# Causal attention in a decoder kernel: the row maximum from half the products, two heads side by side in the array

## The chip, the cores and the metric

One Trainium2 chip, one core. The metric is the device time of one execution in microseconds (us); smaller is better. The kernel is a whole decoder pass of six layers; the change touches one of them, the causal self-attention.

## The reference, cut to what matters

```python
B, S, D, H, DH = 2, 1024, 256, 16, 16
q, k, v = (xn @ Wqkv + bqkv) split by head          # xn: layer norm of x
score = einsum('bhqd,bhkd->bhqk', q, k) * DH ** -0.5
score = where(causal, score, -inf)                  # tril
p = softmax(score)                                  # float32
x = x + (p @ v) @ Wout + bout
```

A softmax row may be shifted by any number near its maximum without changing what it gives, apart from rounding; the kernel uses that below.

## The kernel before

Products in float32 accuracy are made from bf16 parts. Each of q and k is split into three bf16 parts that add up to the float32 value (high, middle, low), and six of the nine part products are kept. `Q_PART` and `K_PART` list them, and the parts of one head are stacked under each other in 6 x 16 = 96 partitions, so that one bf16 matmul with 96 rows sums all six.

The work goes in 8 steps: a step is one batch and a quad of 4 heads. A step does three things.

1. Pieces (`piece`, L1422, with the causal mask added on the diagonal block by a 128-column matmul of `ident16` and `future`, L1425). They are the scores with queries on the partitions, made only for the row maximum. For query tile qi (128 queries) and each half of up to 512 keys there is a matmul for each head; a piece fills one PSUM bank of 512 columns, with as many heads in it as fit (4 heads at 128 keys, 2 at 256, 1 at 384 or 512). VectorE takes the maximum (`reduce`, L1583).
2. The shift. VectorE negates the maxima and splits them into two bf16 parts (`split_shift`, L1594 to L1599), TensorE turns them (`turn_shift`, L1432), VectorE copies them to `stage` (L1606), and two DMAs put them into rows 96 and 97 of the q stack (`keep_shift` on SP, L1332), where k has ones.
3. Scores with keys on the partitions (`scores`, L1444, mask L1447), 98 rows, so that the shift is already subtracted; ScalarE's exp (L1543); and the product with v (`values`, L1459: float32, 128 rows by 32 columns, 4 heads side by side in the array). Then `turn_out` (L1468) and `norm` (L1611, L1613). At the end of a batch come `turn_batch` (L1476), `add_bias` (L1619), `project` (L1484) and `finish` (L1625).

The order is written out by hand and is the same on every engine. The unit is one head with 512 columns: a step has 4 x 9 = 36 units of pieces and as many of scores. `count_pieces` sets `upto`: after each score slot the pieces are issued that bring their sum to `done + 36` units, so that the maxima run one whole step ahead of the scores; at the very start it is `11 + 3.5 * done` for the first 10 units, to catch up. Each engine runs its own list in order: TensorE that waits for one thing holds back all that follows.

PSUM has 8 banks: 3 for scores, one for the output of `values`, and a ring of 4 single banks for everything else (pieces, shifts, turned outputs, projections). A tile of the ring is written when the one 4 earlier has been read (`tile`).

The stacks come from DRAM. `loads(n)` on SP issues 12 DMAs of 128 KB for step n, into one of three buffers; the third (`qs[2]`, `ks[2]`) lies in spent weights and needs the projections of the second batch to be done, and a memset of its ones by GpSimd (L1372), which TensorE waits for before the first piece (`k_ones`(2)). The order on SP is: stores of the parts of batch 0; loads(0), loads(1), keep_shift(0), loads(2); then keep_shift(hs) for each half step, and loads(n+2) after the second half of step n. Before the loads of step 3 stand 6 stores of 512 KB, the parts of batch 1.

```python
aim = 11 + 3.5 * done if done < 10 else done + 36
upto.append(max(upto[-1], sum(a <= aim for a in sums)))
```

```python
score = lambda slot: c.bank(slot % SCORES)
out_tile = c.bank(SCORES)
ring_bank = lambda what: c.bank(SCORES + 1 + nth[what] % TILES)
```

Of the kernel before, what the change touches and what calls it, by code (L numbers as in the profile page):

```python
# [1181 lines left out]

def score_pieces():

    out = []
    for qi in range(TT):
        for half, first in enumerate(range(0, (qi + 1) * P, CH)):
            n = min(CH, (qi + 1) * P - first)
            per = min(QUAD, CH // n)
            out += [(qi, first, n, list(range(h, h + per)), half) for h in range(0, QUAD, per)]  # L1190
    return out


def causal_attention_layer(nc, c):
# [10 lines left out]
    SCORES, TILES = 3, 4  # L1205
# [3 lines left out]
    LATER = 6  # L1209
# [21 lines left out]
    def count_pieces():  # L1231

        size = [len(heads) * n / CH for _, _, n, heads, _ in pieces] * STEPS
# [26 lines left out]
    with ExitStack() as ctx:  # L1260
# [3 lines left out]
                                       loaded0=0, loaded1=0, loaded2=0, shifted0=0, shifted1=0, made=0, read=0,  # L1264
                                       max_step=0, parts=0, scored=0, expd=0, av=0, out_copied=0, inv=0))
        set_round(0, s)
        loaded = [s["loaded0"], s["loaded1"], s["loaded2"]]
# [20 lines left out]
        spare = c.weights[:, 0:first].bitcast(BF16).rearrange("p (a h n) -> p a h n", a=2, h=QUAD)  # L1288
        qs = [q_stack[:, 0], q_stack[:, 1], spare[:, 0]]
        ks = [k_stack[:, 0], k_stack[:, 1], spare[:, 1]]  # L1290
# [11 lines left out]
        ring_bank = lambda what: c.bank(SCORES + 1 + nth[what] % TILES)  # L1302

        with nc.Block() as block:

            @block.sync
            def _(sync):
                def loads(n):
                    b, quad = divmod(n, QUADS)
                    a = n % 3  # L1310
                    if n == 2:
                        pr["v_proj"].round = 1
                        sync.wait_ge(*pr["v_proj"](4))
                    if n >= 3:
                        sync.wait_ge(*s["scored"](QUAD * first_group(2 * (n - 2))))
                    by_head = lambda ap: ap.rearrange("(h d) n -> d h n", d=DH)
                    rows = slice(quad * QUAD * DH, (quad + 1) * QUAD * DH)
                    for r in range(len(Q_PART)):
                        sync.dma_start(qs[a][r * DH:(r + 1) * DH], by_head(q_dram[b, Q_PART[r], rows, :]))\
                            .then_inc(loaded[a].sem, 16)  # L1320
                        sync.dma_start(ks[a][r * DH:(r + 1) * DH], by_head(k_dram[b, K_PART[r], rows, :]))\
                            .then_inc(loaded[a].sem, 16)

# [4 lines left out]
                def keep_shift(hs):  # L1328
                    _, _, half = part_of(hs)
                    sync.wait_ge(*s["read"](nth["shift", hs] + 1))  # L1330
                    for i in range(SHIFT):
                        sync.dma_start(qs[hs // 2 % 3][ROWS + i:ROWS + i + 1, :, half * CH:(half + 1) * CH],  # L1332
# [7 lines left out]
                loads(0)  # L1340
                loads(1)
                keep_shift(0)
                loads(2)
                for hs in range(1, HALVES):
                    keep_shift(hs)
                    if hs == 3:
                        for n in range(2):
                            sync.wait_ge(*s["later_part"](4 * (n + 1)))
                            for i in range(3):
                                store(1, n, i, s["later_stored"])  # L1350
                    if hs % 2 == 1 and 3 <= hs // 2 + 2 < STEPS:
                        if hs // 2 + 2 == QUADS:
                            sync.wait_ge(*s["later_stored"](6 * 16))
                        loads(hs // 2 + 2)

            @block.gpsimd
            def _(pool):
# [11 lines left out]
                pr["v_proj"].round = pr["q_raw"].round = pr["k_raw"].round = 1  # L1369
# [3 lines left out]
                pool.wait_ge(*s["stored"](6 * 16))  # L1373
                pool.wait_ge(*s["k_ones"](2))
# [11 lines left out]
            def _(pe):  # L1386
# [21 lines left out]
                def tile(what):  # L1408
# [3 lines left out]
                    return ring_bank(what)  # L1412

                def piece(p):
                    n, i = divmod(p, NPC)
                    qi, first, keys, heads, _ = pieces[i]
                    if i == 0:
                        pe.wait_ge(*loaded[n % 3](LOADS * (n // 3 + 1)))
                    bank = tile(("piece", p))
                    diagonal = first + keys == (qi + 1) * P  # L1420
                    for x, h in enumerate(heads):
                        mm = pe.matmul(bank[:, x * keys:(x + 1) * keys], qs[n % 3][0:ROWS, h, qi * P:(qi + 1) * P],  # L1422
                                       ks[n % 3][0:ROWS, h, first:first + keys], start=True, stop=not diagonal)
                        if diagonal:
                            mm = pe.matmul(bank[:, (x + 1) * keys - P:(x + 1) * keys], ident16[:], future[:], start=False, stop=True)  # L1425
                    mm.then_inc(s["made"].sem)

                def turn_shift(hs):
                    rows = tile(("shift", hs))[0:SHIFT * QUAD, :].bitcast(BF16)
# [5 lines left out]
                def scores(slot):  # L1435
                    (hs, ki), h = groups[slot // QUAD], slot % QUAD
                    a, half = hs // 2 % 3, hs % 2
                    if ki == 0 and h == 0:
                        pe.wait_ge(*shifted[hs % 2](SHIFT * 16 * (hs // 2 + 1)))
# [24 lines left out]
                def turn_out(hs):  # L1464
                    bank = tile(("out", hs))
# [5 lines left out]
                def turn_batch(b, x):  # L1471
                    m, half = divmod(x, 2)
                    bank = tile(("turn", b, x))
# [5 lines left out]
                def project(b, x):  # L1479
                    m, j = divmod(x, NCH)  # L1480
                    bank = tile(("project", b, x))
# [12 lines left out]
                pe.wait_ge(*s["k_ones"](2))  # L1494
# [64 lines left out]
            def _(dve):  # L1559
# [20 lines left out]
                def reduce(p):  # L1580
                    qi, _, keys, heads, part = pieces[p % NPC]
                    nh = len(heads)
                    dve.tensor_reduce(mx[:, part, qi, heads[0]:heads[0] + nh],  # L1583
                                      tile(("piece", p))[:, 0:nh * keys].rearrange("p (h n) -> p h n", n=keys), AX, ALU.max)\
                       .then_inc(s["read"].sem)
# [66 lines left out]
        clear_signals(nc, norm_s, pr, s)  # L1652

# [778 lines left out]
```

## Time and profile before

| | |
|---|---|
| time, median of 3 runs | 1981.68 us (1981.13 to 1981.76) |
| the profiled execution: time / span | 1980.98 us / 1979.3 us |
| TensorE (PE) busy | 1722.5 us, 87% of the span |
| VectorE (DVE) busy | 901.5 us, 46% |
| ScalarE (ACT) busy | 628.3 us, 32% |
| pieces, L1422 and L1425 | first at 978.96 us, last at 1232.9 us |
| end of the causal layer's last score | 1262 us |

The times of the trace are from the start of the span. Busy shares over the whole span say little here, since the change touches about 285 us of 1979; the rows below are cut to that stretch. A matmul's duration in the trace includes its way through the array, so matmuls overlap in the list: what one costs in a dense stream is the distance from its start to the start of the next. "128*32" after a matmul is its number of rows and columns in the array, "x4" the number of records; a float32 matmul has two records.

### The profile page before, as it was taken

The numbers are of one execution on the slowest core, as the hardware profiler recorded it, in microseconds if no ns is written. First come the engines' busy times: TensorE is split into PE (matmuls) and PEld (weight loads), VectorE is DVE, ScalarE is ACT, GpSimd is POOL, SyncE is SP. The second block draws the span as 40 slices with busy tenths as digits, with TensorE's granted clock in tenths as the row PEclk, the third lists the DMA queues.
The fourth block names the chain that finished last, engine by engine and source line by source line (L and its number), as shares of the span: only waits on it lengthen the run. The fifth ranks groups of instructions, "written<-read, shape, count | busy, mean of one in ns | idle before, by whom it ended". The sixth has DMA issues, their size and how long they took to land. (4 is left out here: it accounts for less than half of the span.)

```text
span 1979.3 us, 20127 instructions
## 1 busy us (share of the span) xinstructions
PE 1722.5 (87%) x7698; PEld 961.8 (49%) x7698; DVE 901.5 (46%) x1458; ACT 628.3 (32%) x1024; POOL 63.6 (3%) x73
## 2 busy tenths in 40 slices
PE   5797795989999977887799999778866999999998
PEld 3444442443222213333445544335643788888886
DVE  3404404664443323122488777154636636354552
ACT  2312312522222223113247656432323322121220
POOL 0000000000000000003220000000002000000000
PEclk8898897989999998998989999989968999999999
DMA  4001000000000000000626240000021022222201
GB/s 171 0 0 58 0 0 3 0 1 0 1 1 1 0 0 0 0 0 0 128 33 129 34 56 11 4 0 1 0 86 57 1 86 85 86 86 86 85 29 43
DMA packets 27693, 67.48 MB, mean 34 GB/s; under 512 B 3096, under 2 KB 14424, under 8 KB 25176
## 3 DMA queue, kind: packets, MB, share of 16 engines
q1 hardware_dynamic: 27608, 66.33, 12.4%
q8 instruction: 55, 0.90, 0.2%
q14 instruction: 30, 0.25, 0.0%
HBM read 57.80 MB, written 8.39 MB: 33 GB/s over the span
## 5 line engine op out<-in xcount | busy, mean ns | idle before, releaser
L1543 ACT ACTIVATE arena<-psum 128x512 f32<-128x512 f32 (+3 forms) x384 | 164.3, 499 | 123.7 <-PE psum L1447 91.6
L1583 DVE TENSOR_REDUCE b_mx<-psum 128x1 f32<-128x512 f32 (+3 forms) x304 | 181.4, 653 | 45.1 <-PE psum L1425 34.4
L2077 PE MATMUL psum<-m_wo,m_hidden 128*128 128x256 f32 (+1 forms) x704 | 153.4, 379 | 1.0 <-DVE arena L2280 1.0
L2175 ACT ACTIVATE m_gelu<-psum 128x512 f32<-128x512 f32 (+1 forms) x88 | 52.5, 597 | 305.2 <-PE psum L2063 305.2
L2077 PEld LDWEIGHTS psum<-m_wo,m_hidden 128*128 128x128 f32 (+1 forms) x704 | 133.7, 190 | 19.3 <-issue 1.2
L2063 PE MATMUL psum<-m_x_high,m_w_high 128*128 128x512 f32 (+1 forms) x352 | 140.0, 398 | 2.9 <-issue 2.9
L2063 PE MATMUL psum<-m_x_rest,m_w_high 128*128 128x512 f32 (+1 forms) x352 | 138.9, 395 | 0.0
L2063 PE MATMUL psum<-m_x_high,m_w_rest 128*128 128x512 f32 (+1 forms) x352 | 138.5, 393 | 0.0
L874 ACT ACTIVATE x_probs<-psum 128x1024 f32<-128x1024 f32 x64 | 65.5, 1023 | 219.2 <-PE psum L730 219.2
L950 DVE TENSOR_REDUCE x_mx<-psum 128x2 f32<-128x1024 f32 x64 | 77.4, 1223 | 116.6 <-PE psum L704 115.9
L2299 DVE TENSOR_TENSOR m_hidden<-m_gelu,psum 128x512 f32<-128x512 f32 (+1 forms) x88 | 60.5, 687 | 139.5 <-PE psum L2063 139.5
L1444 PE MATMUL psum<-b_q_stack,b_k_stack 98*128 98x512 bf16 (+3 forms) x288 | 91.5, 334 | 7.4 <-DMA b_q_stack<-b_stage 3.0
L1422 PE MATMUL psum<-b_k_stack,b_q_stack 96*128 96x512 bf16 (+3 forms) x288 | 90.3, 345 | 6.1 <-POOL weights_sb L1372 3.7
L743 PE MATMUL psum<-x_probs,arena 128*64 128x512 f32 x256 | 69.1, 617 | 9.8 <-ACT x_out L884 9.8
L2063 PEld LDWEIGHTS psum<-m_x_high,m_w_high 128*128 128x128 f32 (+1 forms) x352 | 65.1, 185 | 19.9 <-issue 3.7
L730 PE MATMUL psum<-arena 64*128 64x512 f32 x256 | 73.2, 649 | 0.0
L2063 PEld LDWEIGHTS psum<-m_x_high,m_w_rest 128*128 128x128 f32 (+1 forms) x352 | 65.1, 185 | 16.4
L2063 PEld LDWEIGHTS psum<-m_x_rest,m_w_high 128*128 128x128 f32 (+1 forms) x352 | 65.1, 185 | 16.2
L1459 PE MATMUL psum<-arena,weights_sb 128*32 128x512 f32 (+3 forms) x768 | 71.7, 492 | 0.0
L414 PE MATMUL psum<-arena,weights_sb 128*128 128x512 f32 x128 | 58.6, 621 | 14.2 <-DVE arena L201 14.2
L704 PE MATMUL psum<-arena 64*128 64x512 f32 x256 | 68.1, 623 | 2.9 <-DVE x_mx L950 1.9
L1109 PE MATMUL psum<-weights_sb 128*128 x96 | 48.9, 635 | 18.0 <-PEq L1087 12.2
(375 smaller groups left out, 2678.9 us busy)
## 6 DMA issues: line engine op xcount, KB each, us to landing
m_w<-w SPq DMA_DIRECT2D x16, 1368.0 KB, 9.1
m_wo<-wo SPq DMA_DIRECT2D x8, 1280.0 KB
weights_sb<-weights SPq DMA_DIRECT2D x2, 2820.0 KB, 9.1
b_q_stack<-b_q_dram SPq DMA_DIRECT2D x36, 128.0 KB, 7.0
b_k_stack<-b_k_dram SPq DMA_DIRECT2D x36, 128.0 KB, 7.5
weights_sb<-weights SPq DMA_DIRECT2D x1, 3328.0 KB, 13.1
b_q_dram<-b_q_parts SPq DMA_DIRECT2D x6, 512.0 KB, 3.3
b_k_dram<-b_k_parts SPq DMA_DIRECT2D x6, 512.0 KB, 4.4
```

The costliest lines, as they stand in the source:

```text
L704: mm = pe.matmul(to[:, h * CH:(h + 1) * CH], qt[b][rows, m, q0:q0 + P], kt_[b][rows, m, first:first + CH], start=True, stop=True)
L730: mm = pe.matmul(to[0:keys, h, :], k, qt[b][rows, m, half * CH:(half + 1) * CH], start=False, stop=True)
L743: mm = pe.matmul(out_tile[h * DH:(h + 1) * DH, :], v, probs[slot % RING][0:keys, h, :], start=(kt == 0), stop=(kt == TT))
L874: ins = act.activation(probs[slot % RING][:], two_heads(units), ACT.Exp, scale=SCALE)
L950: dve.tensor_reduce(mx[:, n % 2, i // 2, i % 2, :], two_heads(tile(("piece", n, i))), AX, ALU.max).then_inc(s["read"].sem)
L1422: mm = pe.matmul(bank[:, x * keys:(x + 1) * keys], qs[n % 3][0:ROWS, h, qi * P:(qi + 1) * P], ks[n % 3][0:ROWS, h, first:first + keys], st ...
L1444: mm = pe.matmul(score(slot)[:, 0:n], ks[a][0:ROWS + SHIFT, h, ki * P:(ki + 1) * P], qs[a][0:ROWS + SHIFT, h, q0:q0 + n], start=True, stop ...
L1459: mm = pe.matmul(out_tile[h * PAD:(h + 1) * PAD, CH - n:CH], v_aug[:, b * TT + ki, quad * QUAD + h, :], probs[(QUAD * (2 * pair + i) + h) ...
L1543: act.activation(probs[slot % RING][:, 0:n], score(slot)[:, 0:n], ACT.Exp, scale=SCALE).then_inc(s["expd"].sem)
L1583: dve.tensor_reduce(mx[:, part, qi, heads[0]:heads[0] + nh], tile(("piece", p))[:, 0:nh * keys].rearrange("p (h n) -> p h n", n=keys), AX, ...
L2063: mm = pe.matmul(c.bank(base + n % 2)[0:H_N(h), :], of[:, k, at], x_of[:, k, :], start=(k == 0 and of is w_high[w] and x_of is x_high), st ...
L2077: mm = pe.matmul(bank[:, q * D:(q + 1) * D], hidden[0:H_N(h), h, (2 * i + q) * P:(2 * i + q + 1) * P], wo[0:H_N(h), h, :], start=(h == 0), ...
```

## The change

- For the pieces only three of the six part products are kept (high x high, high x middle, middle x high): 3 x 16 = 48 rows. Scores keep all six.
- Two heads of a pair are computed side by side: one from partitions 0 to 47, one from partitions 64 to 111, each as a matmul of 48 rows, into two different banks. A piece is now a tile of two banks with one pair of heads (2 x 512 or 2 x 384 columns) or two pairs (at 256 or 128 keys). There are 20 pieces in a step in place of 38. The mask on the diagonal is added as before, by one full matmul for each head.
- The ring has 2 tiles of two banks in place of 4 of one bank; shifts, turned outputs and projections take such a tile too and use one bank of it.
- The maximum is taken from both banks by one instruction (up to 128 x 1024).
- The 48-row stacks are loaded on their own (`firsts(n)`: 12 DMAs of 64 KB), with two buffers in spent weights and in `c.ln`. The 96-row stacks now have two buffers (`stacks(n)`: 12 DMAs of 128 KB); GpSimd's memset of the third is gone. The order on SP: firsts(0), stacks(0), keep_shift(0), stacks(1), firsts(1), then after the second half of step n: stacks(n+1), firsts(n+2). Step 3's stores stay where they were.
- `LATER`, the number of pieces between the last piece of a half step and its `turn_shift`, is 3 in place of 6.

```diff
-Q_PART = (0, 0, 0, 1, 1, 2)
-K_PART = (0, 1, 2, 0, 1, 0)
+Q_PART = (0, 0, 1, 0, 1, 2)
+K_PART = (0, 1, 0, 2, 1, 0)
+FIRST = 3
...
-            per = min(QUAD, CH // n)
-            out += [(qi, first, n, list(range(h, h + per)), half) for h in range(0, QUAD, per)]
+            out += [(qi, first, n, pairs, half) for pairs in (((0,), (1,)) if 2 * n > CH else ((0, 1),))]
...
-    SCORES, TILES = 3, 4
+    SCORES, TILES = 3, 2
+    SIDE = P // 2
...
-    LATER = 6
+    LATER = 3
...
-        size = [len(heads) * n / CH for _, _, n, heads, _ in pieces] * STEPS
+        size = [2 * len(pairs) * n / CH for _, _, n, pairs, _ in pieces] * STEPS
...
-        ring_bank = lambda what: c.bank(SCORES + 1 + nth[what] % TILES)
+        ring_tile = lambda what: c.psum[2 + nth[what] % TILES]
+        ring_bank = lambda what: ring_tile(what)[:, 0:CH]
...
+                def firsts(n):
...
+                    if n == 1:
+                        pr["v_proj"].round = 1
+                        sync.wait_ge(*pr["v_proj"](4))
+                    if n >= 2:
+                        sync.wait_ge(*s["made"](nth["piece", NPC * (n - 1) - 1] + 1))
...
+                    for r in range(FIRST):
+                        for y in range(2):
+                            to = slice(y * SIDE + r * DH, y * SIDE + (r + 1) * DH)
+                            sync.dma_start(q_first[a][to], by_side(q_dram[b, Q_PART[r], rows, :])[y]).then_inc(loaded_first[a].sem, 16)
+                            sync.dma_start(k_first[a][to], by_side(k_dram[b, K_PART[r], rows, :])[y]).then_inc(loaded_first[a].sem, 16)
...
-                loads(0)
-                loads(1)
+                firsts(0)
+                stacks(0)
                 keep_shift(0)
-                loads(2)
+                stacks(1)
+                firsts(1)
...
-                pool.wait_ge(*pr["v_proj"](4))
-                pool.wait_ge(*s["k_ones"](1))
-                pool.memset(ks[2][ROWS:ROWS + SHIFT], 1.0).then_inc(s["k_ones"].sem)
...
-                    for x, h in enumerate(heads):
-                        mm = pe.matmul(bank[:, x * keys:(x + 1) * keys], qs[n % 3][0:ROWS, h, qi * P:(qi + 1) * P],
-                                       ks[n % 3][0:ROWS, h, first:first + keys], start=True, stop=not diagonal)
+                    for x, pair in enumerate(pairs):
+                        for y in range(2):
+                            rows = slice(y * SIDE, y * SIDE + FIRST * DH)
+                            mm = pe.matmul(to[:, y * CH + x * keys:y * CH + (x + 1) * keys], q_first[a][rows, pair, qi * P:(qi + 1) * P],
+                                           k_first[a][rows, pair, first:first + keys], start=True, stop=not diagonal)
                         if diagonal:
-                            mm = pe.matmul(bank[:, (x + 1) * keys - P:(x + 1) * keys], ident16[:], future[:], start=False, stop=True)
+                            for y in range(2):
+                                last = y * CH + (x + 1) * keys
+                                mm = pe.matmul(to[:, last - P:last], ident16[:], future[:], start=False, stop=True)
...
+                    of = ring_tile(("piece", p))[:].rearrange("p (y n) -> p y n", y=2)
...
+                    dve.tensor_reduce(to, of, AX, ALU.max).then_inc(s["read"].sem)
```

## Rows read from the trace of the kernel before

The stretches below give, after their length, the busy us of PE, PE's weight loads, DVE, ACT and GpSimd (with instructions), then the granted clock of PE (1.00 is 2.4 GHz), the DMA share and GB/s.

**Rows 1.** Busy time by engine over one whole step of scores.

```profile
1068.39:1099.84 31.45, 31.14 (x277) 15.74 (x273) 25.17 (x49) 21.15 (x50) 0.00 (x0) 1.00 0.42 52
```

**Rows 2.** Groups by line over three such steps, 1036.95 to 1131.28 us.

```profile
L1422 PE MATMUL psum<-b_k_stack,b_q_stack 96*128 96x512 bf16 (+3 forms) x96 | 29.1, 327 | 0.0
...
L1425 PE MATMUL psum<-b_future,b_ident 128*128 128x128 bf16 x96 | 18.6, 220 | 0.0
...
L1422 PE MATMUL psum<-weights_sb 96*128 96x512 bf16 (+3 forms) x48 | 14.5, 326 | 0.0
```

**Rows 3.** PE in order of time inside a step: start, duration, instruction.

```profile
1103.16 0.22 PE L1425 MATMUL psum<-b_future,b_ident 128*128 128x128 bf16 x1
1103.31 0.39 PE L1432 MATMUL psum<-b_ident,b_shift 128*8 128x128 bf16 x4
1103.63 0.34 PE L1444 MATMUL psum<-b_q_stack,b_k_stack 98*128 98x384 bf16 x1
1103.80 0.22 PE L1447 MATMUL psum<-b_past,b_ident 128*128 128x128 bf16 x1
1103.86 0.33 PE L1422 MATMUL psum<-b_k_stack,b_q_stack 96*128 96x384 bf16 x1
...
1110.36 0.38 PE L1422 MATMUL psum<-b_k_stack,b_q_stack 96*128 96x512 bf16 x1
...
1111.24 0.38 PE L1422 MATMUL psum<-b_k_stack,b_q_stack 96*128 96x512 bf16 x1
```

**Rows 4.** PE in order of time in the cross-attention layer, which has matmuls in row halves.

```profile
521.53 0.39 PE L725 MATMUL psum<-x_shift_t,x_ones 2*128 2x512 bf16 x2
521.85 0.70 PE L730 MATMUL psum<-arena 64*128 64x512 f32 x2
...
522.39 0.60 PE L730 MATMUL psum<-arena 64*128 64x512 f32 x2
522.82 0.60 PE L704 MATMUL psum<-arena 64*128 64x512 f32 x2
...
523.25 0.59 PE L704 MATMUL psum<-arena 64*128 64x512 f32 x2
523.77 0.65 PE L743 MATMUL psum<-x_probs,arena 128*64 128x512 f32 x2
```

**Rows 5.** DVE's maxima: over two banks (cross attention) and over one.

```profile
L950 DVE TENSOR_REDUCE x_mx<-psum 128x2 f32<-128x1024 f32 x64 | 77.4, 1223 | 116.6 <-PE psum L704 115.9
...
L1583 DVE TENSOR_REDUCE b_mx<-psum 128x1 f32<-128x512 f32 x72 | 46.1, 680 | 10.5 <-PE psum L1425 7.6 <-PE psum L1422 2.9
```

**Rows 6.** The start of the layer's pieces, GpSimd and DVE in order of time.

```profile
975.33 0.69 DVE L1573 COPY weights_sb<-psum 128x512 f32<-128x512 f32 x1 [1.03 <-PE psum L1404]
975.35 3.51 POOL L1372 MEMSET weights_sb<- 2x4096 bf16 x1 [35.66 <-PE psum L1404]
...
979.62 6.14 DVE L1583 TENSOR_REDUCE b_mx<-psum 128x4 f32<-128x512 f32 x11 [3.60 <-PE psum L1425]
...
994.40 13.31 DVE L1583 TENSOR_REDUCE b_mx<-psum 128x4 f32<-128x512 f32 x23 [0.35 <-PE psum L1425]
...
1008.26 1.28 DVE L1583 TENSOR_REDUCE b_mx<-psum 128x4 f32<-128x512 f32 x2
```

**Rows 7.** SP's queue at the start: first load, first shift.

```profile
954.99 0.33 SPq L1319 DMA_DIRECT2D b_q_stack<-b_q_dram  x1
...
988.41 1.42 SPq L1332 DMA_DIRECT2D b_q_stack<-b_stage  x2
```

**Rows 8.** The stretch in which loads(2) moves, columns as in Rows 1.

```profile
989.87:1003.30 13.43, 11.48 (x54) 5.28 (x55) 10.79 (x19) 3.86 (x7) 13.10 (x5) 0.73 0.97 118
```

**Rows 9.** The stretch in which loads(3) moves, columns as in Rows 1.

```profile
1050.00:1062.70 12.70, 12.70 (x101) 6.15 (x103) 11.76 (x23) 9.85 (x21) 0.00 (x0) 1.00 1.05 176
```

**Rows 10.** PE's waits for DVE at turn_shift, 1040 to 1170 us (total, times, longest).

```profile
PEld psum L1432 <- DVE b_mx L1583: 2.6, 8, 0.5
```

**Rows 11.** DVE in the layer's tail.

```profile
1267.62 2.73 DVE L1619 TENSOR_SCALAR arena<-psum,vectors_sb 128x512 f32<-128x512 f32 x4 [0.81 <-PE psum L1476]
```

More of the change, by code:

```diff
@@ L1339, in _ @@
                 sync.wait_ge(*s["stored"](6 * 16))
-                loads(0)
-                loads(1)
+                firsts(0)
+                stacks(0)
                 keep_shift(0)
-                loads(2)
+                stacks(1)
+                firsts(1)
                 for hs in range(1, HALVES):
                     keep_shift(hs)
+                    n = hs // 2
                     if hs == 3:
[L1347 to L1352, printed above, removed]
+                        for i in range(2):
+                            sync.wait_ge(*s["later_part"](4 * (i + 1)))
+                            for part in range(3):
+                                store(1, i, part, s["later_stored"])
+                    if hs % 2 == 1:
+                        if 2 <= n + 1 < STEPS:
+                            stacks(n + 1)
+                        if n + 2 == QUADS:
                             sync.wait_ge(*s["later_stored"](6 * 16))
-                        loads(hs // 2 + 2)
+                        if n + 2 < STEPS:
+                            firsts(n + 2)
             @block.gpsimd
@@ L1464, in turn_out @@
                 def turn_out(hs):
-                    bank = tile(("out", hs))
+                    bank = tile(("out", hs))[:, 0:CH]
                     pe.wait_ge(*s["out_copied"](hs + 1))
@@ L1472, in turn_batch @@
                     m, half = divmod(x, 2)
-                    bank = tile(("turn", b, x))
+                    bank = tile(("turn", b, x))[:, 0:CH]
                     pe.wait_ge(*s["read"](nth["out", 2 * QUADS * (b + 1) - 1] + 1))
@@ L1480, in project @@
                     m, j = divmod(x, NCH)
-                    bank = tile(("project", b, x))
+                    bank = tile(("project", b, x))[:, 0:CH]
                     pe.wait_ge(*s["read"](nth["turn", b, 3] + 1))
@@ L1580, in reduce @@
                 def reduce(p):
[L1581 to L1585, printed above, removed]
+                    qi, _, keys, pairs, part = pieces[p % NPC]
+                    dve.wait_ge(*s["made"](nth["piece", p] + 1))
+                    of = ring_tile(("piece", p))[:].rearrange("p (y n) -> p y n", y=2)
+                    if len(pairs) == 1:
+                        of, to = of[:, :, 0:keys], mx[:, part, qi, 2 * pairs[0]:2 * pairs[0] + 2]
+                    else:
+                        of = of[:, :, 0:2 * keys].rearrange("p y (x n) -> p y x n", x=2)
+                        to = mx[:, part, qi, :].rearrange("p (x y) -> p y x", y=2)
+                    dve.tensor_reduce(to, of, AX, ALU.max).then_inc(s["read"].sem)
                 def split_shift(hs):
```

52 lines of the change are left out of this document (29 added, 23 removed).

## The prediction

> **What bounds the layer now.** I read the busy time of one whole step first, cut out from one first score to the next. A step takes 31.45 us; PE is busy 31.14 of it, DVE 25.17, ACT 21.15 [rows 1]. So PE sets the pace, with hardly a gap, and its clock is full; what DVE or ACT saves is worth nothing here until DVE needs over 31 us. Then I read the groups of three such steps: the pieces are 144 matmuls (96 and 48), 48 in a step, and 96 masks, 32 in a step [rows 2]. By the code these 48 carry 36 units of 512 columns.
>
> What PE's instructions cost is their distance in order of time, and not their duration. Four 512-column matmuls start within 1111.24 - 1110.36 = 0.88 us, 0.22 us each; a 128-column one passes in 0.06 us (1103.80 to 1103.86) [rows 3]. A step's pieces are thus 36 x 0.22 = 7.9 us plus 32 x 0.06 = 1.9 us of masks.
>
> **What the change takes away on PE.** A head has 48 rows, and two heads run side by side. Cross attention shows such a pair: the two halves (records x2) of a 512-column bf16 matmul are followed after 0.32 us, and 0.10 of that is another matter, below, so both pass in the 0.22 us of one [rows 4]. 36 units become 18: -3.95 us per step. Masks are full matmuls still, one for each head: no change.
>
> **What it adds on PE: a change of shape in the array.** Wherever the array goes from one division to another, an extra shows:
> - Full to narrow columns, bf16 on both sides: mask to turn_shift 0.15 us (1103.16 to 1103.31) against 0.06: +0.09. Back: 0.32 us for four transposes of 0.056 to 0.06: +0.09 [rows 3].
> - Row halves, float32: L730 to L704, halves on both sides, 0.43 us; L704 to L743, from row halves to full rows, 0.52 us: +0.09. From the 2-row bf16 pair to 64-row pairs 0.32 against 0.22: +0.10 [rows 4].
>
> No row shows a bf16 step from 128 rows to 48 or back. Its bounds are 0 and 0.10; every change of shape in the rows, four kinds of them, costs 0.09 to 0.10, so I take 0.095, and 0.19 to 0.20 for going in and out. How often? In a step there are 8 diagonal and 4 other key spans, two pairs of heads in each: 24 pairs. The masks (full) follow each diagonal pair, also between the two pairs of a four-head piece, and by the written order a score or a mask stands between any two pieces. So 24 entries and 24 exits: 24 x 0.19 to 0.20 = +4.6 to +4.8 us. Net +0.6 to +0.9 us per step; I take +0.75. The point from which it turns is 3.95 / 24 = 0.165 us for in and out together. It is the narrow pairs that lose: a 128-column pair saves 0.06 us and pays 0.19; even a 512-column pair gains only 0.03.
>
> The Trainium skill (TensorEngine Tiling (Array Packing), "Key Properties") says that a change of tiling mode, and not just of tile, drains TensorE. By that rule the charge falls on all 48 changes, as in the sum; by its table "Theoretical Speedup" (up to 2 times for a contraction of at most 64) alone the pieces would gain 3.95 us per step with nothing to pay, the first rival. Rows 4 agree with both, the pair in the time of one and the 0.09 at the border.
>
> It counts where PE sets the pace: the pieces of steps 2 to 7 and some 0.7 of step 1's, 6.7 steps: 6.7 x 0.75 = +5.0 us.
>
> **The ring of two.** DVE's reading of two banks is 1.22 us against 0.68 for one [rows 5]. By durations a step's maxima cost now 30 x 0.68 and 8 (at 384 columns) x some 0.55, 24.8 us, and afterwards 14 of 1024 columns, 4 of 768 and 2 of 512: 14 x 1.22 + 4 x 0.95 + 2 x 0.68 = 22.3 (0.95 and 0.55 lie on the line through the two rows). So DVE's 25.2 us [rows 1] become some 22.7: further from the bound, and worth nothing by itself. But the ring is two deep, and turn_shift must have the tile two back. In the half with full spans the order is: 512-wide pair, score, four-head piece at 128 keys, turn_shift. From the end of the wide pair PE gets there after 0.22 + (0.38 changes + 4 x 0.06 masks + 2 x 0.06) = 0.96 us; DVE needs the matmul's way through the array (0.22 - 0.06 = 0.16 us [rows 3]) and 1.22, 1.4 in all: PE waits about 0.4 to 0.5 us, and by the same count in the other half, where it now waits 2.6 / 8 = 0.3 us each time [rows 10]. So +0.2 each, +0.4 per step; bounds are 0 (ACT lags behind in that half, and what PE loses to DVE it would lose to ACT anyway) and 1.2 (DVE late by one more tile). LATER at 3 two-unit pieces is the same lead as before. I take +0.3: 6.7 x 0.3 = +2.0 us.
>
> The tail and the end of batch 0 use the ring for 4 turns and 4 projections each. There four evictions run back to back in 2.73 us, 0.68 each [rows 11]. With two tiles each turn waits for the read two back, while DVE is at the next: nothing lost if PE fills a tile within 0.68 us, 0.2 if it needs its four transposes and the way through on top. Over 16 of them that is 0 to 3 us; I take +1.0.
>
> **The start.** PE's first piece waits for GpSimd's memset, until 975.35 + 3.51 = 978.86 us [rows 6]. The memset is gone; what is left is DVE's last copy of the projection, 975.33 + 0.69 = 976.02 [rows 6]: -2.8 us. firsts(0), 0.79 MB, starts at 954.99 [rows 7] and at the 118 GB/s of loads(2) [rows 8] is there by 962; stacks(0), 1.57 MB more, by 976, before the first score: both hidden by the projections.
>
> That lead is lost again at the first piece of step 1. DVE sets the pace here: 11, 1, 3 and 23 maxima, the last ending at 994.40 + 13.31 = 1007.71, and step 1 begins at 1008.26 [rows 6], from loads(1), which had come long before. After the change that data is firsts(1), which SP issues behind keep_shift(0) and stacks(1). The first shift goes out at 988.41 [rows 7], afterwards some 2.6 earlier, 985.8; the issue of the stacks from 987.3. loads(2) moved 1.57 MB in 13.4 us [rows 8]; 2.36 MB take 20.1: landed at 1007.4. DVE would want the pieces 2.8 and some 0.4 for fewer maxima before 1007.71, at 1004.5. So PE stands still in front of them for 3 to 4 us, the scores behind it too, and DVE's first maximum of step 1 is at about 1008.3, where it is now. I take +0.3 for what is over (a bound of -2.8 if the two loads overlap better than that, of +3 if the standstill brings the clock down, as the 0.73 of rows 8 shows that this stretch can).
>
> **Later loads.** In a plain step SP issues 24 DMAs in place of 12, 20 us of data, and the next shift's two DMAs queue behind them; from keep_shift of the second half (some 6 units into the next step's pieces) to the next step's scores there are 30 of 36 units, 26 us, so they fit. Only once do the 6 stores come first: loads(3) moves until 1062.70 [rows 9], and in its place stacks(2) and firsts(3) will, the second after the first. 0.79 MB more take 6.7 us: 1069.4, and keep_shift(4) behind it, wanted where the stretch of rows 1 begins, at 1068.39, plus the delay so far. +0.6 us; bounds 0 and 3.
>
> **Sum.** 5.0 + 2.0 + 1.0 + 0.3 + 0.6 = +8.9 us: 1980.98 becomes 1989.9 for the profiled execution, whose span is 1979.3; the median of the runs is 0.7 higher, so 1990.5. Layers after the causal one are only moved.
>
> **Rivals.**
> - Faster, "the change of shape is cheap for bf16 rows": the side-by-side pair keeps its 3.95 us and in and out cost less than 0.165. For it: no row has just this change. Against: four kinds of change all cost the same. If in and out cost 0.10 together: 24 x 0.10 = 2.4, net -1.55 per step, -10.4, and with the other +3.9 the median is 1981.7 - 6.5 = 1975; at nothing the step would be 27.5 us, which DVE's 22.7 allows: 1981.7 - 26.5 + 3.9 = 1959. Chance 0.10.
> - No difference (1977.7 to 1985.6; 0.2%, 4 us, is about what a measurement of this kernel can tell from no change): the changes of shape fall into PE's waits for ACT, which already make some of the step, the ring waits too, and the start keeps part of its 2.8. Step net +0.2 and +1 elsewhere: 1984. Chance 0.15.
> - Slower by more, "the ring is the new bound": each shift waits 0.6 us more, and double pieces hold back scores so that ACT then lacks work: +1.5 a step in place of 0.3, +8: 1998.5. For it: DVE is at 80% in a step [rows 1], and a tile's read holds PE up nearly twice as long [rows 5]. Against: it has slack on average, and the lead of PE in units is the same. Chance 0.20.
> - Forecast: 0.55, own range 1986 to 1995.
>
> Slower 0.75, same 0.15, faster 0.10. The range leaves out most of the faster case and the end of the ring case: 1981 to 2001.
>
> **What the profile afterwards should show.** The pieces' matmuls x384 as 48*128, in pairs that start together; 0.31 us from a 512-wide pair to the next full matmul, 0.15 from a mask to the next pair. Maxima x160 with a mean near 1.1 us. A step of 32.2 to 32.8 us with PE busy over 98%. The first piece at 976; a stand of PE before the first piece of step 1, released by firsts(1). turn_shift waiting for DVE by 0.5 us. The prediction is wrong if a pair to mask takes 0.22 us flat (the first rival), or if a step is over 33.5 us with waits for DVE (the third).

## The result

The changed kernel takes 2007.24 us (median of 4 runs, 2005.85 to 2008.62) against 1981.72 us before: ratio 1.0127 [1.0109, 1.0144], +25.5 us. Forecast were 1990.5 us and a range of 1981 to 2001: the sign was right, the size nearly three times too small. The profiled execution took 2005.85 us, its span is 2004.2 us, +24.9.

Where the 24.9 us lie, by the starts of the steps' first scores (before, after). The first row ends where DVE starts its last copy out of the projection, with which the layer's pieces can begin:

| stretch | before | after | difference |
|---|---|---|---|
| up to the last copy, unchanged code | 975.3 | 972.8 | -2.5 |
| from there to the first score of step 1 | 61.6 | 69.1 | +7.5 |
| steps 1 to 6 (six steps) | 199.7 | 218.9 | +19.1 |
| step 7, scores without pieces | 25.3 | 25.3 | 0.0 |
| the rest of the kernel | 717.2 | 718.0 | +0.8 |

The -2.5 us are not the change's: the trace of run 4, with the same loads, has that copy at 974.77, that of run 2 at 974.64 (rows 6: 975.33). The changed kernel's:

```profile
972.83 0.69 DVE L1605 COPY weights_sb<-psum 128x512 f32<-128x512 f32 x1 [1.03 <-PE psum L1430]
```

A plain step has 34.5 us in place of 31.45 [rows 1]: +3.05, where the forecast's terms give 0.75 and 0.3. First the changes of shape. PE in order of time at the beginning of a step, and at one pair of 512 columns:

```profile
1076.43 0.39 PE L1476 MATMUL psum<-b_q_stack,b_k_stack 98*128 98x512 bf16 x1
1076.65 0.22 PE L1479 MATMUL psum<-b_past,b_ident 128*128 128x128 bf16 x1
1076.81 0.23 PE L1451 MATMUL psum<-weights_sb 48*128 48x128 bf16 x2
1076.97 0.29 PE L1456 MATMUL psum<-b_future,b_ident 128*128 128x128 bf16 x2
1077.19 0.23 PE L1451 MATMUL psum<-weights_sb 48*128 48x128 bf16 x2
...
1077.97 0.22 PE L1479 MATMUL psum<-b_past,b_ident 128*128 128x128 bf16 x1
1078.12 0.28 PE L1451 MATMUL psum<-weights_sb 48*128 48x256 bf16 x2
1078.34 0.29 PE L1456 MATMUL psum<-b_future,b_ident 128*128 128x128 bf16 x2
...
1095.82 0.39 PE L1451 MATMUL psum<-weights_sb 48*128 48x512 bf16 x2
1096.14 0.39 PE L1476 MATMUL psum<-b_q_stack,b_k_stack 98*128 98x512 bf16 x1
```

From a mask to the pair in row halves there are 0.16 and 0.15 us where rows 3 had 0.06; from a 128-column pair to the masks 0.16 in place of 0.06, from a 256-column pair 0.22, from a 512-column pair 0.32, where one matmul takes 0.11 and 0.22. So the change costs 0.09 to 0.11 us each way. The pair passes in the time of one matmul: from 256 to 512 columns the distance grows by 0.10 us, and not by twice that. That step of the forecast was right, for the form that no row had shown.

And then the waits. The same busy times as in rows 1, and the waits of PE's weight loads for DVE from 1040 to 1170 us (total, times, longest):

```profile
1076.48:1110.97 34.49, 32.65 (x276) 13.16 (x274) 24.47 (x32) 21.57 (x50) 0.00 (x0) 1.00 0.54 70
```

```profile
PEld psum L1451 <- DVE b_mx L1621: 7.3, 20, 0.6
...
PEld psum L1463 <- DVE b_mx L1621: 3.4, 7, 0.5
```

Neither PE nor DVE is at its limit: PE is busy 32.65 of 34.49 us (95% in place of 99%), DVE 24.47. The weight loads wait at the pieces (L1451) and at turn_shift (L1463) together 10.7 us in these 130 us, where rows 10 had 2.6 for the shifts; part of that passes while a matmul is still running. Inside a step it looks like this:

```profile
1096.14 0.39 PE L1476 MATMUL psum<-b_q_stack,b_k_stack 98*128 98x512 bf16 x1
1096.77 0.66 PE L1500 MATMUL psum<-ident,ln 128*128 128x128 f32 x4 [0.24 <-DVE b_mx L1621]
1097.27 0.38 PE L1476 MATMUL psum<-b_q_stack,b_k_stack 98*128 98x512 bf16 x1
1097.90 0.39 PE L1451 MATMUL psum<-weights_sb 48*128 48x512 bf16 x2 [0.26 <-DVE b_mx L1621]
```

turn_out (L1500) starts 0.63 us after a score that passes in 0.22, and the next piece again 0.63 us after one, which with 0.09 for the shape would be 0.31: 0.4 and 0.3 us of waiting for tiles that DVE has not read. The groups of DVE in this step:

```profile
L1621 DVE TENSOR_REDUCE b_mx<-psum 128x2 f32<-128x1024 f32 x12 | 14.6, 1221 | 5.5 <-PE psum L1456 3.7 <-PE psum L1451 1.8
L1621 DVE TENSOR_REDUCE b_mx<-psum 128x2 f32<-128x768 f32 x4 | 3.7, 953 | 2.1 <-PE psum L1456 2.1
```

The durations are those expected (1.22 us as in rows 5, 0.95). DVE is idle for 10.0 of the 34.49 us of the same step in which PE waits for it: too little room between the two, not too little speed.

The start, where DVE's reading had set the pace. PE in order of time, DVE's first maximum of step 1, and PE over 997 to 1007 us:

```profile
1003.13 0.40 PE L1456 MATMUL psum<-b_future,b_ident 128*128 128x128 bf16 x2
1007.30 0.29 PE L1451 MATMUL psum<-weights_sb 48*128 48x128 bf16 x2 [3.78 <-DMA weights_sb<-b_k_dram]
```

```profile
1008.50 0.69 DVE L1621 TENSOR_REDUCE b_mx<-psum 128x4 f32<-128x512 f32 x1 [3.08 <-PE psum L1456]
```

```profile
997.00:1007.00 10.00, 6.52 (x30) 1.85 (x28) 8.20 (x11) 2.35 (x5) 0.00 (x0) 0.50 0.95 118
```

The standstill in front of firsts(1) is there, until 1007.3 (forecast: 1007.4), and DVE takes up step 1 at 1008.50 (forecast 1008.3; before 1008.26 [rows 6]); counted from the layer's last copy that is 2.7 us later than before. What was foreseen only as a bound comes with it: the granted clock stands at its lower level, 1.2 GHz, from 977.5 to 1018.4 us without a break, 41 us; before there were 3.4, 10.2 and 3.4 us of it in this stretch. From DVE's first maximum of step 1 to the first score of the next half step there are 10.2 us (1008.5 to 1018.7) in place of 7.6.

### The profile page after: what moved, and what is told of

It is laid out like the page before. It is cut to its first block and busy times, and to the rows that moved or that the text cites. A ratio compares the mean times of both kernels' runs of the same rounds, so it can differ in the third digit from the quotient of the medians.

```text
span 2004.2 us, 20079 instructions
## 1 busy us (share of the span) xinstructions
PE 1733.5 (86%) x7698; PEld 938.9 (47%) x7698; DVE 898.2 (45%) x1314; ACT 631.0 (31%) x1024; POOL 60.2 (3%) x72
## 5 line engine op out<-in xcount | busy, mean ns | idle before, releaser
L1621 DVE TENSOR_REDUCE b_mx<-psum 128x2 f32<-128x1024 f32 (+3 forms) x160 | 174.0, 1114 | 75.3 <-PE psum L1456 57.9
L874 ACT ACTIVATE x_probs<-psum 128x1024 f32<-128x1024 f32 x64 | 65.5, 1024 | 219.2 <-PE psum L730 219.2
L1476 PE MATMUL psum<-b_q_stack,b_k_stack 98*128 98x512 bf16 (+3 forms) x384 | 114.4, 338 | 10.1 <-ACT arena L1575 5.0
L1476 PEld LDWEIGHTS psum<-b_q_stack,b_k_stack 98*128 98x128 bf16 x384 | 35.8, 98 | 71.7 <-issue 40.0
```

Of the source, the lines that this page charges most:

```text
L874: ins = act.activation(probs[slot % RING][:], two_heads(units), ACT.Exp, scale=SCALE)
L1476: mm = pe.matmul(score(slot)[:, 0:n], ks[a][0:ROWS + SHIFT, h, ki * P:(ki + 1) * P], qs[a][0:ROWS + SHIFT, h, q0:q0 + n], start=True, stop ...
L1621: dve.tensor_reduce(to, of, AX, ALU.max).then_inc(s["read"].sem)
```

## The experiments

All times are beside runs of the kernel before on the same chip (medians 1978.98 to 1980.87). "Step" is the distance from first score to first score of a plain step. Runs 1, 2, 5, 6, 7, 9, 10, 11 ask what fills it; 3, 4, 5, 8, 12 are about the start.

**Run 1, the ring alone.** The kernel before with the two-bank tiles, 96-row products and old loads.

```diff
-    SCORES, TILES = 3, 4
+    SCORES, TILES = 3, 2
...
-    LATER = 6
+    LATER = 3
...
+                    for x, pair in enumerate(pairs):
+                        for y in range(2):
+                            mm = pe.matmul(to[:, y * CH + x * keys:y * CH + (x + 1) * keys], qs[n % 3][0:ROWS, 2 * pair + y, qi * P:(qi + 1) * P],
```

> The kernel before with only the ring changed: tiles of two banks, two of them, one maximum over both banks, LATER 3. The 96-row products, one head after the other, and the loads stay as before, so there is no change of shape and no late load. Theory, that the ring of two makes 1.7 us of waits in each step by itself: a step of 32.8 to 33.2 us in place of 31.44, 1991 to 1995 us. Rival, that the waits come only because the pieces in row halves arrive in another rhythm: a step of 31.4 to 31.7, 1981 to 1984 us.

Measured: 2000.97 us, ratio 1.0106 [1.0089, 1.0123], a step of 34.05 us. The rival is out: with no matmul in row halves at all, the tiles and their order cost 2.6 us in each step, more than the 1.7 of the theory and most of the 3.05. The waits have the same places as in the changed kernel.

**Run 2, row halves with single banks.** Each item of the ring counts its banks (`bank_of`, `read_by`), a piece two, all others one.

```diff
+    for what in order:
+        bank_of[what] = at
+        at += 2 if what[0] == "piece" else 1
+        read_by[what] = at
...
-                    if n >= TILES:
-                        pe.wait_ge(*s["read"](n - TILES + 1))
+                    if read_by[what] > TILES:
+                        pe.wait_ge(*s["read"](read_by[what] - TILES))
```

> The changed kernel with the ring counted in single banks again, four of them: a piece takes two, shifts, turned outputs and projections one; DVE reads each bank by an instruction of its own. Row halves and loads stay. Theory of the ring: PE's waits at turn_shift, turn_out and the wide pieces go, a step of 32.4 to 33.0 us in place of 34.50 (31.44, plus 1.0 for the changes of shape), 1994 to 1998 us. Rival, that DVE's speed and not the depth of the ring holds PE up: with DVE's two reads no faster than one, a step of 34 or more, 2004 or more.

Measured: 2000.83 us, 1.0105 [1.0088, 1.0121], a step of 33.39 us. The depth of the ring gives back 1.1 us of a step, less than expected; 1.95 over the kernel before remain.

**Run 3, firsts(1) before stacks(1).**

```diff
-                stacks(1)
                 firsts(1)
+                stacks(1)
```

> The changed kernel with firsts(1) issued before stacks(1). Theory, that the late load costs the standstill and the clock after it: firsts(1) lands at about 995, PE does not stand still at 1003, the first score of step 1 comes at 1037 to 1038 in place of 1041.97, 2002 to 2004 us. Rival, that the clock stays low in this stretch because PE has less to do in row halves: the standstill goes but the clock stays at half, and 1 to 2 us are won, 2005 to 2006.

Measured: 2003.23 us, 1.0122 [1.0105, 1.0138]; the ratios don't tell it from the changed kernel (1.0127), the traces do. The standstill is gone, the first score of step 1 comes at 1038.6 in place of 1041.9. But the clock did not come back with it. 997 to 1007 us, before and in this run:

```profile
997.00:1007.00 10.00, 8.62 (x56) 3.66 (x54) 10.00 (x18) 3.04 (x7) 6.05 (x3) 1.00 0.68 75
```

```profile
997.00:1007.00 10.00, 9.77 (x52) 3.31 (x50) 9.21 (x13) 2.73 (x6) 0.00 (x0) 0.50 1.08 120
```

PE is busy 98% of this stretch and is granted half the clock, from 977.6 to 1015.1. Each theory was half right: the standstill cost 3.3 us (both traces have the layer's last copy within 0.13 us of each other), the low clock is not its consequence.

**Run 4, GpSimd's split after the first shift's parts.** As run 3, and one wait more on GpSimd:

```diff
+                pool.wait_ge(*s["parts"](1))
```

> As the one with firsts(1) before stacks(1), and GpSimd starts to split batch 1 only after the first shift's parts. Theory, that DVE's small instruction L1633 took 3.12 us in place of 0.17 because GpSimd was in a long one: it takes 0.2 us, the first score comes 2.5 to 3 us earlier than in the run without it, 1999 to 2002 us. Rival, that the first score waits for something else (loads of the stack) or the time is lost again before step 1: no difference from it.

Measured: 2004.17 us, 1.0124 [1.0107, 1.0141], no better than run 3. The first score came 12.7 us after the layer's last copy, at 987.5, in place of run 3's 15.7: the 2.9 us that were expected. But the first score of step 1 came 65.7 us after the copy, as in run 3 (65.6): the hold-up had moved. DVE's and GpSimd's instructions at the two places, first in the changed kernel, then in this run:

```profile
980.06 4.05 POOL L1409 TENSOR_TENSOR b_k_parts<-arena,b_k_parts 128x2048 bf16<-128x2048 f32 x1
```

```profile
981.02 3.12 DVE L1633 TENSOR_SCALAR b_shift<-b_mx 128x16 bf16<-128x16 f32 x1
```

```profile
1003.74 4.06 POOL L1410 TENSOR_TENSOR b_k_parts<-arena,b_k_parts 128x2048 bf16<-128x2048 f32 x1
```

```profile
1003.86 3.98 DVE L1631 TENSOR_TENSOR b_mx<-b_mx 128x16 f32<-128x16 f32 x1
```

Both of DVE's instructions work on 128x16 numbers and take 0.17 us otherwise; both end within 0.05 us of the end of GpSimd's (984.11 and 984.14, 1007.80 and 1007.84). DVE's maxima out of PSUM keep their length: nine of them take 10.00 us beside GpSimd in this run (from 993.82), and 10.00 without it in the changed kernel (from 994.79). The Trainium skill (SBUF — State Buffer, "Terms") calls this a port pair that DVE and GpSimd share and that one holds for its full instruction; the trace agrees.

**Run 5, full rows.** As run 3, with matmuls over 112 rows.

```diff
-                            rows = slice(y * SIDE, y * SIDE + FIRST * DH)
+                            rows = slice(0, SIDE + FIRST * DH)
```

> The changed kernel with firsts(1) early, whose pieces run over 112 rows, both heads' parts at once, one matmul after the other: no change of shape and nothing side by side. It leaves out the separation of the two heads (each maximum is that of the sum of two heads' products), so its numbers differ; the number and width of the matmuls is that of the 96-row pieces. Theory, that a step is the sum of ring and shapes: 34.05 us, as with the ring alone. Clock: if it is the row halves that keep it at half speed at the start of the layer, it rises at about 1000 us as with the ring alone; if it is the order of the start, it stays at half until 1015.

One run, 1997.56 us, without an interval; a step of 34.05 us, that of run 1 to the hundredth, so that the loads and their buffers play no part in it. The clock rose at 993.1 and stayed up for the rest of the stretch:

```profile
997.00:1007.00 10.00, 7.31 (x54) 3.71 (x52) 9.90 (x13) 3.11 (x7) 5.64 (x2) 1.00 1.08 120
```

and from the first score of step 0 to that of step 1 there are 46.4 us, 3.5 less than run 3's 50.0. In the runs with row halves the clock stayed low until 1015 to 1025 (changed kernel, runs 2, 3, 4, 7, 10), in those with full rows until 993 to 1001 (runs 1, 5, 6, 8, 9, 11, 12 and the kernel before, some of them with one dip of 3.4 us soon after). Full rows also pass twice as many columns one after the other, so what about the row halves keeps the clock low is not shown.

**Run 6, the order alone.** Run 1 with run 2's single banks: pairs of heads in full rows, four banks.

```diff
-    SCORES, TILES = 3, 2
+    SCORES, TILES = 3, 4
...
-        ring_bank = lambda what: ring_tile(what)[:, 0:CH]
+        ring_bank = lambda what, y=0: c.bank(SCORES + 1 + (bank_of[what] + y) % TILES)
```

> The kernel before with pieces of a pair of heads, LATER 3 and the order that follows, but with four single banks and one maximum for each bank: what the coarser order costs without the shallow ring and without row halves. Run 2 of this study (row halves, single banks) stood at 33.39 us a step, of which 1.0 is shape: if order and coarse release cost the rest, this one has 32.2 to 32.5 us, 1984 to 1988 us. Rival, that waits and shapes don't add: 31.5, 1979 to 1981 us.

Measured: 1994.51 us, 1.0069 [1.0052, 1.0085], a step of 33.02 us: above what the theory gave. Coarse pieces cost 1.6 us a step without a shallow ring and without row halves. And row halves, from here to run 2, add 0.37 us and not 1.0; from run 1 to the changed kernel 0.45. The 1.0 is 24 x 0.205 us for the changes less the 3.95 that the pairs save. Some 0.6 us of it don't show; they may fall where PE would wait anyway (its weight loads wait 3.7 us for ACT in run 1's step, 2.7 in the changed kernel's), but no run takes this apart.

**Run 7, masks first.** Run 2 with firsts(1) early; the masks are written before the products, so that a piece of two pairs enters row halves once. A product on the diagonal is now written in two parts, which makes 576 matmuls of pieces in the layer in place of 384.

```diff
+                    if diagonal:
+                        for x in range(len(pairs)):
+                            for y in range(2):
+                                pe.matmul(to[y][:, (x + 1) * keys - P:(x + 1) * keys], ident16[:], future[:], start=(x == 0), stop=False)
+                    for x, pair in enumerate(pairs):
+                        for a0, n0 in ((0, keys - P), (keys - P, P)) if diagonal else ((0, keys),):
```

> The changed kernel with single banks, firsts(1) early, and the masks written before the products: a piece of two pairs goes into row halves once and not twice, 20 entries in a step in place of 24. Theory of the shapes: 4 x 0.205 = 0.8 us less than 33.39, a step of 32.6 us, 1992 to 1996 us. Rival, that the changes of shape are hidden behind waits by now: 33.3 to 33.4.

Measured: 1992.24 us, 1.0061 [1.0044, 1.0078], a step of 32.46 us: 0.93 less than run 2, expected were 0.8. The changes of shape fall by 12 in a step and not by 8, from 63 to 51 with those to narrow columns counted, since in four places narrow matmuls now follow the row halves at once. At 0.1 us each that is 1.2 us: at these places, the narrow pieces, most of the price is paid. Masks and products changed places with it, which was not tried alone.

**Run 8, the memset off the path.** The kernel before; TensorE waits for `k_ones`(1) at its first piece and for `k_ones`(2) at the first score of step 2.

```diff
+                        if hs == 4:
+                            pe.wait_ge(*s["k_ones"](2))
...
-                pe.wait_ge(*s["k_ones"](2))
+                pe.wait_ge(*s["k_ones"](1))
```

> The kernel before, whose first piece no longer waits for GpSimd's memset of the third stack's ones; TensorE waits for it at the first score of step 2 instead. Theory, that this is the part of the change that gains: the first piece at 976.1 in place of 978.96 us, loads(0) and loads(1) are there, so step 1 comes 2 to 2.8 us earlier, 1976 to 1977.5 us on a chip where the kernel before takes 1979 (its own ratio 0.9986 to 0.999). Rival, that DVE's small instruction waits for GpSimd until the same time as before: the first score at 991 and no gain.

Measured: 1978.86 us (10 runs) against 1980.67: 0.9991 [0.9981, 1.0001], not to be told from no change by this. In its trace the first piece starts at 975.43 and the first score of step 1 at 1032.7, 4.2 us earlier, and the last score 4.2. Of these, 0.8 us lie before the layer (its last copy starts at 974.48), 3.4 are the layer's. The layers after it then took 721.1 us in place of 717.2. The same code took 717.2 to 721.1 in this study's traces; between these two nearly all of it arises from 1414 to 1500 us, where one wait of PE for DVE (L2119) has 13.2 us in place of 10.1. Why it differs stays open.

**Run 9, waits bank by bank.** Run 6, with a wait for each bank in front of its own matmul.

```diff
+                            if x == 0 and bank_of["piece", p] + y + 1 > TILES:
+                                pe.wait_ge(*s["read"](bank_of["piece", p] + y + 1 - TILES))
```

> The kernel of run 6 (pairs of heads, full rows, four single banks, 33.02 us a step) where TensorE waits for each bank of a pair when it comes to write it, and not for both before the first. Theory, that the wait for two free banks out of four is what the pairs cost: a step of 31.6 to 32.2 us. Rival, that it is the coarse order (two units at once, with a score's wait on ACT behind them): 32.8 to 33.0.

Measured: 1990.31 us, 1.0044 [1.0030, 1.0059], a step of 32.47 us: between the two. The wait for two free banks is 0.55 us of the 1.58.

**Run 10, four heads at once.** Run 7, with both pieces of a key span issued together, all masks first.

```diff
-                upto.append(max(upto[-1], sum(a <= aim for a in sums)))
+                upto.append(max(upto[-1], whole(sum(a <= aim for a in sums) - 1) + 1))
...
-                    tile(("piece", p))
+                    tile(("piece", ps[-1]))
```

> The kernel of run 7 (row halves, single banks, masks first, 32.46 us a step) where all four heads of a key span are issued together: 12 entries into row halves in a step in place of 20, but each needs all four banks free. By the shapes alone 8 x 0.205 = 1.6 us less, 30.8 us a step, 1978 to 1982 us. Theory, that coarse pieces cost waits: they come back as 1.5 to 3 us more, 32.5 to 34 us a step, 1991 to 2003 us.

Measured: 2032.48 us, 1.0254 [1.0237, 1.0272], steps of 35.2 to 38.4 us: worse than the theory. Fewest changes of shape and most of the waiting. One of its steps:

```profile
1087.72:1126.10 38.38, 33.55 (x299) 14.51 (x298) 25.50 (x51) 21.63 (x50) 0.00 (x0) 0.91 0.49 63
```

PE has 4.8 us of holes, and a clock of 0.91; it falls for a while in five of the steps 1 to 6.

**Run 11, two at a time.** The kernel before with another `upto`: pieces only in whole pairs of heads.

```diff
-        upto, done = [pieces_upto(0) + 1], 0.0
+        upto, done = [pieces_upto(0) + 2], 0.0
...
-                upto.append(max(upto[-1], sum(a <= aim for a in sums)))
+                fit = sum(a <= aim for a in sums)
+                upto.append(max([upto[-1]] + [w for w in whole if w <= fit]))
```

> The kernel before, unchanged but for the list that says after which score how many pieces are issued: they come two heads' units at a time, as in the changed kernel. One head in a bank, each bank with its own signal, wait and maximum. If the coarse order alone is the cost: 32.5 to 33.0 us a step. If it is what a pair waits for and signals (both banks free, both products done): 31.4 to 31.8 us a step and no change in time.

Measured: 1983.14 us, 1.0011 [1.0001, 1.0021], a step of 31.79 us, +0.35. The coarse order alone is the small part. From here to run 9, 0.68 us, lies what is left of a pair when its banks are waited for one by one: DVE hears of it only when both heads are done, and LATER is 3 pairs of heads. Four heads at 128 keys also take two banks in place of one (320 maxima in the layer in place of 304).

**Run 12, the best version.** Run 8, and GpSimd splits q after the parts of half step 0 and k after those of half step 2.

```diff
                     pool.wait_ge(*ready(4))
+                    pool.wait_ge(*s["parts"](2 * n + 1))
                     pool.tensor_copy(parts[:, 0, :, :], raw)
```

> The kernel of run 8 (before, with the memset off the path), and GpSimd splits batch 1's q only after the parts of the first half step and its k after those of the third. Theory, that DVE's small instructions wait for the end of GpSimd's long ones: the 1.93 us of L1599 become 0.17, the first score comes at 986.4 in place of 988.2, and no other of DVE's small ones is held up: 1.5 to 2 us faster than run 8, 0.2% to 0.3% faster than the kernel before. Rival, that the block moves to another place as in run 4: the time of run 8.

Measured: 1976.72 us (9 runs) against 1980.87, 0.9976 [0.9966, 0.9986]: the only one faster than the kernel before, by 0.24%. DVE's small instruction at the start:

```profile
982.44 0.18 DVE L1600 TENSOR_SCALAR b_shift<-b_mx 128x16 bf16<-128x16 f32 x1
```

It takes 0.18 us (1.20 before, 1.93 in run 8), the first score comes at 986.6, 4.4 us earlier than before (3.7 counted from the layer's last copy), and the first of step 1 at 1032.6, no earlier than in run 8: inside the layer the two differ by 0.1 us at its end, so what this second edit adds is not shown. It carries over what in the change was good, and leaves the pieces alone.

## Why the prediction was wrong

A step's 3.05 us, taken apart by the runs. Each line is a step's busy time as in rows 1: run 11, run 9, run 6, run 1.

```profile
1067.09:1098.88 31.79, 31.24 (x276) 15.64 (x272) 25.19 (x50) 21.27 (x50) 0.00 (x0) 1.00 0.40 51
```

```profile
1068.26:1100.73 32.47, 31.62 (x277) 15.62 (x274) 25.41 (x52) 21.49 (x50) 0.00 (x0) 1.00 0.40 50
```

```profile
1071.93:1104.95 33.02, 31.89 (x277) 15.42 (x274) 25.50 (x52) 21.53 (x50) 0.00 (x0) 1.00 0.39 49
```

```profile
1072.70:1106.75 34.05, 31.95 (x277) 15.50 (x274) 24.48 (x32) 21.58 (x50) 0.00 (x0) 1.00 0.38 48
```

| what comes in | step | adds |
|---|---|---|
| before | 31.44 | |
| pieces issued in pairs of heads (run 11) | 31.79 | 0.35 |
| a pair is signalled once; LATER 3; four heads at 128 keys in two banks (run 9) | 32.47 | 0.68 |
| a pair waits for both its banks (run 6) | 33.02 | 0.55 |
| two tiles of two banks (run 1) | 34.05 | 1.03 |
| row halves (the changed kernel) | 34.50 | 0.45 |

DVE's busy time is 24.5 to 25.5 in all of them: it is never the bound. PE's weight loads wait for it, summed over the lines of a step, 0.8 us before, then 0.9, 1.9, 2.7 and 3.7, and 3.7 again with the row halves. The first line, run 11's 0.35 us, is not among these waits: there the waits for ACT grow, from 2.1 to 4.2 us.

- **What bounds the layer.** Right: PE. But that DVE had slack on average was taken to mean that it holds nobody up. Its work comes in bursts, and the depth of the ring is what evened them out (1.03 us a step from run 6 to run 1). Nor did it shrink as forecast: 24.47 us a step are left of 25.17, and not 22.7. The forecast took the difference of durations, and these did fall by 2.5 us, from 27.8 to 25.3 a step for all of DVE's instructions. But instructions that follow each other overlap, by 2.7 us in a step before and by 0.9 after, with fewer of them.
- **The ring of two.** This is the step that failed, and it is a term of wrong size. The prediction's own sign, a step over 33.5 us with waits for DVE, came true. +0.3 us a step was taken, from a walk through two places (the shifts), with 0 and 1.2 as bounds. Measured are 1.03 for the ring itself and 2.6 with the coarse pieces that it comes with. The walk looked at the wait of one item behind one item; turn_out and the wide pieces, which wait just the same, were not walked through, and the pair as a unit (one signal, two free banks at once) was costed at nothing. "The lead of PE in units is the same" was the wrong sentence: the units are the same, the items are half as many.
- **The changes of shape.** The price and the count were right, 0.09 to 0.11 us and 48. Their net +0.75 a step came out as +0.45; that part of it falls into waits is likely and not shown. In run 7, 12 changes less give back 0.93 of some 1.2 us.
- **The start.** The term was +0.3, with a bound of +3 "if the standstill brings the clock down". Measured are +7.5 us from the layer's last copy to the first score of step 1. Right were the gain at the first piece (0.95 us after the copy starts, 3.63 before) and the 20.1 us for the two loads (issued from 987.30, there at 1007.30). Wrong was that the lead reaches the shift: L1633, held up by GpSimd, takes 3.12 us in place of 0.17, and the first score comes 15.7 us after the copy in both traces. That shift, end of the standstill and DVE's first maximum of step 1 came within 0.2 us of the times forecast is therefore luck: the layers before ended 2.5 us sooner in this trace and made up for the hold-up. In order of time the 7.5 us are 2.7 up to DVE's first maximum of step 1, 2.6 in the half step at the low clock, and 2.1 in the rest (23.2 us in place of 21.1, at full clock), which are step 1's own pieces and were counted with the steps (0.7 x 3.05). By runs, from the first score of step 0 to that of step 1, there are 46.0 us before, 46.4 in run 5, 50.0 in run 3 and 53.4 in the changed kernel: 3.5 us for the standstill, and 3.5 for the row halves, low clock and changes of shape together. The clock was low from 977.5 on, long before the standstill, and in run 3 without one.
- **Later loads, tail.** Nothing stands out: step 1, in which the six stores and the loads behind them move, has 34.5 us like the others (+0.6 was taken). Step 4 with the turns and projections of batch 0 grew by 3.3, 0.25 more than a plain one, step 6 by 3.6, and the tail's four evictions from 2.73 [rows 11] to 2.91 us: some 1 us in all, as taken.
- **The rivals.** The faster one was excluded by the first pair in the trace. The third, "the ring is the new bound", had the mechanism and 0.20; its +1.5 a step was too small as well.
- **The sum.** It gave +8.9 for the profiled execution, and +24.9 was measured, 16.0 more. The ring with its coarse pieces gives (2.6 - 0.3) x 6.7 = +15.4 of that, the row halves -2.0, the start 7.5 - 2.1 - 0.3 = +5.1, and the layers before it -2.5; what is left of the small terms cancels.

Not tried: one signal for a pair, LATER 3 and the second bank at 128 keys each by itself, and a run that separates low clock from row halves by any other means than full rows. Each step time and each place in the start is read from one trace of its run.

## What to carry to other kernels

A shared ring that decouples two engines is to be counted in items and not in bytes: half as many tiles of double size is a shallower ring, even when the engine that empties it has slack (here 25 us of work in a step of 31) and gets a little less to do. Before making two matmuls run side by side, multiply the number of entries into that shape by what the way in and out costs (here 0.19 to 0.2 us) and set it against the columns saved; narrow ones lose. And a small instruction of DVE on SBUF data can last until the end of the GpSimd instruction that it meets. When two traces are compared stage by stage, look first whether they enter the stage at the same time.

## What the runs showed of the hardware

- A bf16 change between full rows and 48-row halves costs 0.09 to 0.11 us each way, and 0.09 to 0.10 do changes of columns and of float32 halves [rows 3, 4].
- With the pieces in row halves the granted clock stayed at 1.2 GHz for 38 to 44 us at the start of the layer (the changed kernel and runs 2, 3, 4, 7, 10), for 10 us of it with PE busy 98% (run 3); with the same number of matmuls in full rows it was 2.4 GHz from 993 to 1001 us on (runs 1, 5, 6). In plain steps it was 1.00 in both, but for run 10.
- DVE instructions of 0.17 us on 128x16 numbers in SBUF took 1.20 (before), 1.93 (run 8), 3.12 (changed kernel) and 3.98 us (run 4), each ending within 0.05 us of a GpSimd instruction of 1.9 to 4.1 us; maxima out of PSUM were not held up.
